# Graph attention layer on one core: a new order of work in the steps of single tiles

## The reference

```python
mask = adj.astype(jnp.float32) + jnp.eye(n, dtype=jnp.float32)
q, k, v = [(h @ W.T + b).reshape(n, 8, 32) for W, b in ((Wq, bq), (Wk, bk), (Wv, bv))]
scores = jnp.einsum('nhd,mhd->hnm', q, k) / jnp.sqrt(32.0)
scores = jnp.where(mask[None] == 0, -1e9, scores)
ctx = jnp.einsum('hnm,mhd->nhd', jax.nn.softmax(scores, axis=-1), v).reshape(n, 256)
h1 = layer_norm(h + ctx @ Wo.T + bo, ln1_g, ln1_b)
h2 = layer_norm(h1 + relu(h1 @ W1.T + b1) @ W2.T + b2, ln2_g, ln2_b)
```

## Time and profile before

| what | value |
|---|---|
| median of 3 runs | 558.27 us (551.36 to 558.89) |
| the profiled execution | 556.26 us, of which the span is 554.5 us |
| PE busy, PEld busy | 87%, 68% of the span |
| DVE, ACT, POOL busy | 77%, 39%, 47% |
| mean granted TensorE clock | 0.937 of full |
| DMA, mean | 254 GB/s |

### The profile page before, as it was taken

One profiled execution on the slowest core, in us unless ns is written; L12 is line 12 of the kernel. 1 busy time (PEld: TensorE's weight loads), 2 busy tenths in 40 slices (PEclk: granted clock), 3 DMA queues, 4 the chain that ended last, 5 costly groups with the idle time before them and its releaser, 6 DMA issues.

```text
span 554.5 us, 7282 instructions
## 1 busy us (share of the span) xinstructions
PE 483.4 (87%) x2274; PEld 376.7 (68%) x2274; DVE 425.2 (77%) x978; ACT 214.5 (39%) x526; POOL 262.3 (47%) x381
## 2 busy tenths in 40 slices
PE   5999999757699899799989989979878888789994
PEld 4888888655458757675875776668435767458883
DVE  0648696998979999999999987869988898550103
ACT  1244343324362463345336255423443143532430
POOL 6444347363633556745754553515625555305133
PEclk9999989999699999989989999978788799799998
DMA  7999868999999798998898785344765842401011
GB/s 278 418 417 418 318 214 330 400 409 420 398 329 351 266 366 261 366 348 287 323 348 318 247 292 187 138 165 148 262 222 163 302 143 58 134 1 39 0 39 42
DMA packets 39771, 140.94 MB, mean 254 GB/s; under 512 B 4904, under 2 KB 16552, under 8 KB 35632
## 3 DMA queue, kind: packets, MB, share of 16 engines
q1 hardware_dynamic: 24608, 95.03, 45.3%
q0 software_dynamic: 13328, 43.55, 22.7%
q10 hardware_dynamic: 1792, 1.85, 1.0%
HBM read 123.61 MB, written 16.80 MB: 253 GB/s over the span
## 4 chain that ended last, share of the span: by engine, by line
PE 51%; DVE 19%; DMA 10%; issue 8%; ACT 6%; POOL 5%; SPq 0%; POOLq 0%; ACTq 0%; DVEq 0%
PE ps L1086 15%; PE ps L1099 12%; PE ps L1719 10%; DVE found L504 6%; DMA xT_all<-in_xT 4%; PE ps L843 2%; PE ps L1066 2%; DMA work<-q_table,row_of 2%; POOL slots L1011 2%; DMA adj_buf<-in_adj 2%; PE ps L846 1%; ACT xT_all L1143 1%; PE ps L1076 1%; DMA early<-in_wqkvT 1%; PE ps L1054 1%
## 5 line engine op out<-in xcount | busy, mean ns | idle before, releaser
L504 DVE FIND_INDEX8 found<-ones,adj_buf 128x8 uint32<-128x4105 int32 (+5 forms) x40 | 138.7, 3467 | 0.0
L1086 PE MATMUL ps<-xT_all,w 128*128 128x512 f32 (+1 forms) x288 | 125.7, 585 | 0.3 <-ACT xT_all L1116 0.2
L1099 PE MATMUL ps<-w,xT_all 128*128 128x256 f32 x512 | 122.7, 395 | 2.9 <-ACT xT_all L1133 1.6
L1099 PEld LDWEIGHTS ps<-w,xT_all 128*128 128x128 f32 x512 | 99.2, 199 | 17.7 <-ACT xT_all L1133 2.7
L1086 PEld LDWEIGHTS ps<-xT_all,w 128*128 128x128 f32 x288 | 56.0, 203 | 47.6 <-issue 44.1
L1011 POOL DMA_INDIRECT slots<-kv_table,col_of x54 | 55.9, 1035 | 48.3 <-DVE col_of L587 36.4
L1133 ACT ACTIVATE xT_all<-ps,col_table 128x512 f32<-128x512 f32 (+1 forms) x72 | 45.8, 642 | 57.1 <-PE ps L1086 52.3
L1719 PE MATMUL ps<-early,xT_all 128*128 128x256 f32 x256 | 60.2, 398 | 6.1 <-DMA early<-in_wqkvT 6.1
L1719 PEld LDWEIGHTS ps<-early,xT_all 128*128 128x128 f32 x256 | 50.7, 200 | 14.2 <-DMA xT_all<-in_xT 4.7
L1153 DVE BATCH_NORM_STATS2 stats<-ps 128x6 f32<-128x256 f32 x62 | 22.1, 418 | 36.5 <-PE ps L1054 36.5
L954 ACT ACTIVATE xT_all<-ps,col_table 128x256 f32<-128x256 f32 (+1 forms) x38 | 14.5, 432 | 84.5 <-PE ps L846 84.5
(11 more groups left out here) (180 smaller groups left out, 821.7 us busy)
## 6 DMA issues: line engine op xcount, KB each, us to landing
adj_buf<-in_adj SPq DMA_DIRECT2D x31, 2048.0 KB
xT_all<-in_xT SPq DMA_DIRECT2D x14, 512.0 KB, 24.5
kv_table<-slots POOLq DMA_DIRECT2D x7, 1024.0 KB, 11.2
slots<-kv_table SPq DMA_DIRECT2D x12, 512.0 KB
q_table<-slots POOLq DMA_DIRECT2D x16, 256.0 KB
out_dram<-early SPq DMA_DIRECT2D x7, 512.0 KB
q_own<-q_table SPq DMA_DIRECT2D x12, 256.0 KB
slots<-in_adj SPq DMA_DIRECT2D x1, 2048.0 KB, 23.0
```

What stands on the lines that cost most here:

```text
L504: last = nc.vector.max_index(dst, ones8[:], part)
L1086: last = nc.tensor.matmul(ps[:, q["bank"] + f % 2, 0:q["g"] * P], w1[:, k, f * P:(f + 1) * P], q["h1T"][:, k, :], start=(k == 0), stop=(k ...
L1099: nc.tensor.matmul(to, q["ffT"][:, f, j * P:(j + 1) * P], w2[:, f, :], start=(f == 0), stop=False)
```

## The change

No instruction is added or dropped; instructions change places in their engine's order, and ff and out tiles change gaps.

- In steps 10 to 16 (the step after next is a single tile) `starts_pe` stands right behind `sum_pe`, ahead of `dense(4)` and `dense(5)`; `sum0_pe` comes behind the sum of step 16 instead of ahead of it, and `ctx0_act` behind `ctx_act`.
- `dense(3)` comes ahead of `post_pe_h1`; `dense(2)` ahead of `tr_pe` in the single steps too.
- The ff of jobs in groups of 4 and 3 steps move into gaps 1 to 4 of places 1 and 2; the out tiles of the job before move too, the last from step 16 to step 15.
- attn's tiles ahead of `lists_pe`: 3 in steps 4 to 10, 2 in other paired steps, 1 in single ones (before: 3 always). attn waits for the residual input only behind its first two products.
- ACT: `post_act_h1_bias` moves from the end of place 0 to behind the mask of place 1; `post_act_x` moves from behind `ctx_act` to ahead of it.

```diff
@@ def sum_pe / sum0_pe
-            if q.b == SUM0:
+            if q.b == SUM0 + 1:
                 pe.wait_ge(ctx0_ready, 1)
...
-            pe.wait_ge(ctx_ready, SUM0)
+            pe.wait_ge(ctx_ready, SUM0 + 1)
@@ def post_pe_attn
                 pe.wait_ge(ctx_sem, ctx_value)
-                pe.wait_ge(q["x_biased"], n + 1)
                 wait(pe, q["ff"], n * FC)
             for j in js:
                 to = tile_out(q, q["bank"], j)
                 for k in range(KC):
                     nc.tensor.matmul(to, q["ctxT"][:, k, j * P:(j + 1) * P], wo[:, k, :], start=(k == 0), stop=False)
+                if j == 0:
+                    pe.wait_ge(q["x_biased"], n + 1)
                 last = add_residual(to, q["xT"], j)
@@ def ff_gap
             if count == 3:
-                return (((), (), (), (), (), (0, 1)), ((2,), (), (3, 4), (5,), (), ()), ((6,), (7,), (), (), (), ()))[place][gap]
-            return (((), (), (), (), (), ()), ((0, 1), (), (2, 3), (4,), (), ()), ((5,), (), (6, 7), (), (), ()), ((),) * 6)[place][gap]
+                return (((),) * 6, ((), (0,), (1, 2), (3, 4, 5), (6,), ()), ((), (7,), (), (), (), ()))[place][gap]
+            return (((),) * 6, ((), (0,), (1, 2), (3, 4), (), ()), ((), (5,), (6, 7), (), (), ()), ((),) * 6)[place][gap]
@@ def outs_own
-            return {(2, 3): (0,), (3, 2): (1,), (3, 3): (2,)}.get((place, gap), ())
+            return {(2, 3): (0,), (3, 2): (1,), (3, 3): (2, 3)}.get((place, gap), ())
@@ def outs_before
-            if count_of(g - 1) < 4:
+            if count_of(g - 1) == 4:
+                return ()
+            if count_of(g) == 2:
                 return {2: (2,), 3: (3,)}.get(gap, ())
-            return {2: (3,)}.get(gap, ())
+            return {3: (2, 3)}.get(gap, ())
@@ ACT, a step
                     mask_act(act, STEPS[i + 1])
+                if place == 1 and n >= 0:
+                    post_act_h1_bias(act, now, n)
...
                 dense(3)
+                if place == count - 1 and q.group < GROUPS - 1:
+                    post_act_x(act, JOBS[q.group], q.group)
+                ctx_act(act, q)
                 if i == SUM0:
                     ctx0_act(act)
-                ctx_act(act, q)
                 dense(4)
                 dense(5)
-                if place == 0 and n >= 0:
-                    post_act_h1_bias(act, now, n)
-                if place == count - 1 and q.group < GROUPS - 1:
-                    post_act_x(act, JOBS[q.group], q.group)
@@ PE, a step
+                ahead = 3 if 0 <= i - SCORE0 < PIECES0 else 2 if q.T > 1 else 1
                 if place == 0 and n >= 0:
-                    post_pe_attn(pe, now, n, ctx_ready, job_ctx_ready(n), (0, 1, 2))
+                    post_pe_attn(pe, now, n, ctx_ready, job_ctx_ready(n), range(ahead))
                 dense(1)
                 if soon:
                     lists_pe(pe, soon)
                 if place == 0 and n >= 0:
-                    post_pe_attn(pe, now, n, ctx_ready, job_ctx_ready(n), (3,))
+                    post_pe_attn(pe, now, n, ctx_ready, job_ctx_ready(n), range(ahead, GROUP))
...
-                if i + 2 < NB and q.T > 1:
+                if i + 2 < NB:
                     dense(2)
                 tr_pe(pe, q)
-                if i + 2 >= NB or q.T == 1:
+                if i + 2 >= NB:
                     dense(2)
+                dense(3)
                 if place == 0 and n >= 0:
                     post_pe_h1(pe, now, n)
-                dense(3)
-                if i == SUM0:
-                    sum0_pe(pe)
                 if i == NB - 1:
                     post_pe_attn(pe, JOBS[GROUPS - 1], GROUPS - 1, ctx_ready, NB - 2)
                 sum_pe(pe, q)
+                single = i + 2 < NB and STEPS[i + 2].T == 1
+                if single:
+                    starts_pe(pe, STEPS[i + 2])
+                if i == SUM0:
+                    sum0_pe(pe)
                 dense(4)
                 dense(5)
-                if i + 2 < NB:
+                if i + 2 < NB and not single:
                     starts_pe(pe, STEPS[i + 2])
```

## The result

| | before | after |
|---|---|---|
| median, same chip | 557.59 us (551.36 to 558.89, 4 runs) | 562.34 us (560.33 to 564.11, 4 runs) |
| ratio, 95% interval | 1 | 1.0108 (1.0064 to 1.0152) |
| span of the profiled execution | 554.5 us | 562.4 us |
| mean granted TensorE clock | 0.937 | 0.929 |

The changed kernel is slower by 1.1%, 3.6 to 8.5 us by the interval, which is within the 2% that counts as no change. 564 was predicted. The ratio stands for 6.0 us, the two medians are 4.8 us apart, and the two profiled executions 7.9 us.

What follows compares the result with a forecast made beforehand. DVE bounds steps 4 to 9, chains between engines 10 to 18, PE step 3 and the tail. +3 (A) - 1.5 (B) + 6 (C to E) = +7.5 on 556.26, about 564 us; likeliest case 558 to 568.

Steps and rivals of the forecast that it cites:

- Part A: Steps 1 and 2: residual input ahead of the context copy makes ACT and PE wait; +3 us, bounds +1.7 to +3.4.
- as at 122.84: Step 2: PE's clock falls after 4.3 us idle, as in the earlier row where four matmuls took 1.69 us; 1.7 more.
- Part B: Paired steps 3 to 9: DVE is full and gives back only its own waits; -1.5 us, bounds 0 and -5.4.
- 142 to 144: Sign that the forecast is right: steps 4 to 9 together take 142 to 144 us.
- Part C: Steps 10 and 11: line 566 of step 11 no longer waits 1.72 us behind post_act_h1_bias; -1.05 us.
- Part D: Steps 12 to 15: lead reaches about -2.3, then ff 5 loses it; step 15 begins 0.4 early, its sum 1.5 late.
- Part E: Steps 16 to 18: late tile 0's sum (+2.5) and two more ff (3.6) make step 18's sum +6 late; bounds +1, +9.
- after 472: Sign that the forecast is right: ACT stays idle for line 970 in step 16 until after 472.
- The first (PE the bound): PE, not DVE, limits the paired steps: -10.4 us in steps 4, 6, 8 and 10, total 555; chance 0.13.
- The second (early offsets shorten the steps): Steps 10 to 18 lose the chain's stalls: -11 us, total 547; chance 0.08.
- The third (lower clock): Steps 16 and 17: idle gaps keep PE's clock low, four of five ff cost 7 more, total 571; chance 0.17.
- The fourth (nothing seen): Step 3's DVE slack of 3.5 us absorbs the early wait, the ff find other gaps; total 556; chance 0.17.

Runs made afterwards that it cites:

- e10: Changed kernel with the residual input's bias behind the copies in step 1 alone and steps 15 to 18 in the order of before; 551.75 us, 0.9927 of before.
- e4: Changed kernel with the residual input's bias behind the copies everywhere and steps 15 to 18 in the order of before; 558.14 us, 1.0021 of before.
- e1: Changed kernel with the residual input's bias back behind the context copy everywhere; 567.74 us, 1.0198 of before.
- e7: Kernel before with dense(3) ahead of h1 in the paired steps and nothing else; 556.65 us, 1.0027 of before.
- e5: Changed kernel with only tile 0's sum and its copy back ahead of step 16's sum and copy; 1.0009 of before.
- e6: Changed kernel with only the last group's ff table as before; 1.0115 of before.
- e2: Changed kernel with tile 0's sum, the last group's ff table and the last out tile as before in steps 15 to 18; 555.25 us, 0.9977 of before.
- e11: Changed kernel with the residual input's bias behind the context copy in step 11 alone; 567.52 us, 1.0231 of before.
- e8: Kernel before without seven of eight products of out tile 3 for four jobs in steps 4 to 10; 557.77 us, 1.0012 of before.
- e9: Changed kernel with the residual input's bias behind the context copy in step 1 alone; 559.35 us, 1.0075 of before.
- e12: e10 with ff 5 of step 14 also back in front of ell; 552.08 us, 0.9892 of before.

## Why the prediction was right, and where it was not

The sum was +7.5 and the span grew by 7.9, but two terms were wrong, D by about 3 us and E by 3.7, in opposite directions. The direction and the mechanisms of A, B and E were right; that the total came so near is in good part luck.

**Part A** (+3) was right in mechanism and size: +3.5 at step 3, +3.9 with this edit alone, and it is there in every kernel that has the bias ahead in step 1 (step 2 lasts 26.1 to 27.9 us) and in none that hasn't (22.5 to 24.9). The clock was to fall as at 122.84 and did; PE idled 5.57 us where 4.3 were forecast. What the part left out is that the same edit helps in the later groups. It said "costs nothing there", and named only what a late input would cost; e10 against e4 (0.9927 and 1.0021, which differ in the bias of steps 3 to 15 alone) puts this at 0.9%, 5 us. Their profiles tell only 0.7 us of that as a wait behind the bias (step 10); most of the rest, 1.7 us in step 11 and 4.6 in step 12, goes with a lower clock in e4 (0.75 against 0.94 in step 12).

**Part B** (-1.5) had the right bound and was small: 141.16 us, 2.7 less, just under the 142 to 144 given. PE's wait moved from h1 (2.93 us) to the sum, as predicted (1.99 us at 241.01 in after), and DVE gave back part of its gaps alone.

**Part C** (-1.05) found the amount but not the place. In step 11 line 566 waits 0.43 instead of 1.72 us, and step 11 lasts 26.31 instead of 26.34: DVE waits the difference one chain link later, for the lists, which stand behind PE's other work.

```profile
342.89 0.48 DVE L566 TENSOR_SCALAR work<-work,spill 128x128 f32<-128x128 f32 x2 [0.43 <-ACT idx_all L907]
...
347.08 0.16 DVE L578 TENSOR_SCALAR row_at<-ps 128x2 f32<-128x2 f32 x1 [2.76 <-PE ps L805]
```

Before, that second wait was 1.76 us. The gain is in step 10 (21.98 to 20.70 us), where line 566 waited 1.18 us behind the bias and now doesn't; e1 and e4, which have it behind, take 21.41 with a wait of 0.62 us, so the bias is worth some 0.7 us of the 1.3.

**Part D** is the step that failed. With part C it let the lead grow by 2.3 us from step 10 to step 14; it grew by 5.3 (1.3 in step 10, 2.9 in step 12, 1.2 in step 13). One cause was in the diff and was not priced: in the single steps one attn tile, not three, stands ahead of the lists. Timeline of step 12, before:

```profile
368.17 2.05 PE L1066 MATMUL ps<-wo,xT_all 128*128 128x256 f32 x4 [0.28 <-issue]
...
370.44 1.92 PE L1066 MATMUL ps<-wo,xT_all 128*128 128x256 f32 x4
...
372.48 1.03 PE L1066 MATMUL ps<-wo,xT_all 128*128 128x256 f32 x4
373.56 0.51 PE L805 MATMUL ps<-idx_all,work 128*128 128x9 f32 x4
...
374.11 0.16 DVE L578 TENSOR_SCALAR row_at<-ps 128x2 f32<-128x2 f32 x1 [3.56 <-PE ps L805]
```

and after:

```profile
366.96 1.09 PE L1065 MATMUL ps<-wo,xT_all 128*128 128x256 f32 x4
...
368.77 0.61 PE L805 MATMUL ps<-idx_all,work 128*128 128x9 f32 x4 [0.51 <-DVE work L566]
```

The wait of 3.56 us is gone; 1.84 us of it come back in DVE's line 1154, which wants all attn tiles (before, no wait). Step 12 went from 25.52 to 22.66 us; in the other kernels with this order and the bias ahead in step 11 it took 23.2 to 24.3. Part of the 2.9 us is the clock, 0.80 before and 0.92 after. At a clock of 0.93 step 12 took 24.97 us with attn as before (e7) and 24.33 (e5, e6, e2) or 23.10 (e11) with the new order; by that the order gives some 0.6 to 1.9 us, an estimate, since the slow stretches do not lie in the same places; at 0.75 the new order took 27.8 (e1, e4), longer than before. No run puts the three tiles back by themselves. The 1.2 us of step 13 were not traced to one cause. Then, as predicted, ff 5 cost the lead at step 14: at 408.12 it took 3.74 us and DVE waited 2.14 us, so that 4.3 became 2.2.

**Part E** (+6 with C and D, 6.4 from the start of step 15) had the right mechanism, and its absolute times were close: line 660 of step 17 was 3.5 late (4.0 by the sum of the parts), sum 17 7.1 (7.5), sum 18 7.9 (7.5), line 970 at 475.67 ("after 472"). But they were reached from a lead 3.3 us greater than forecast, and the stage itself grew by 10.1 us. The sum of step 17 came 54.82 us after the start of step 16, before 44.43: 10.4 later, where the prediction named some 6. The mis-sized term is tile 0's sum: 2.5 us in the forecast, 5.5 by e5. It had 6.6 or 8.5 us for the two halves, and they took 9.2 after the idle time; ACT's wait doubled to 9.45 us. The two further ff, 3.6 us in the forecast, are worth nothing by themselves in e6 and, with the out tile, 0.3% in e2, within the noise. So the split within E was wrong too: the forecast priced the two ff only where they arrive, ahead of step 17's sum, and put nothing on the place that they leave, ahead of the distances, where DVE waits 3.1 us more in e6.

**The rivals.** The first (PE the bound) fell with e7 and e8. The second (early offsets shorten the steps) was right in part for steps 10 to 13, helped by the clock, and wrong for 16 to 18, for the reason it named, the in-order wait in `ctx0_act`. The third (lower clock) is at work inside part E: 0.80 in step 16 and 0.73 in step 17, where before had 1.00 and 0.84. It wasn't as dear as 571, because only between one and two of the five ff were slow: 11.48 us is 9 and 2.5 more, and a slow one costs 1.8. The fourth (nothing seen) fell: the wait in step 2 was not absorbed.

## What to carry to other kernels

An instruction that waits for a DMA holds all that its engine has queued behind it, so the same move can cost where the input is just in time and pay where it has long landed: here it is best split by group (e10, 0.9927). Before pricing a reordering, go through every instruction that now stands between a product and its consumer in each kind of step, also the ones the change lifts out of the way: the wait of 3.56 us in step 12 was one that the prediction had not listed. Price a moved instruction both where it arrives and where it leaves (e6). And before a longer stage is put down to the order, compare its granted clock: e1 and e11 have one order in step 12 and 4.7 us between them.

## What was not expected of the hardware

The same order can run at different clocks in the same place. Up to step 12, after, e2, e5 and e6 have the same order, and step 12 took 22.66, 24.34, 24.33 and 24.33 us; e1 and e4 on one side and e11 on the other have one order in it, and took 27.8 and 23.10; the executions of one kernel spread over 3 to 8 us (before from 552.61 to 560.18 in one series). A shift of a few us early in the kernel was seldom found whole at the end: e9 won 5.0 us by step 3 and 3.2 at sum 18, e12 won 1.7 us in step 14 and lost 1.4 in the steps behind. And 1.33 us of ACT's time moved in step 11 (e11) cost 1.2% of the whole, with no stage in its profile that accounts for it; this is the one result here for which no cause was found.
